# A four-layer decoder on one core: the first self attention's step order, and the last mixture's gather and buffers

## The reference, cut to what matters

```python
# first block: 16 heads of 64 features; x = x + this(layernorm(x))
q, k, v = x @ W_Q + b_Q, x @ W_K + b_K, x @ W_V + b_V      # per head
out = softmax(q @ k.T / 8) @ v;  out = sum over heads of out @ W_O + b_O

# last block: 32 experts, each takes its best cap = 70 of 1792 tokens
xe = xf[idx]                                   # gather: 70 tokens per expert
gate, upv = split(xe @ w_up.T)                 # 256 + 256 features
ye = (silu(gate) * upv) @ w_down.T
out = zeros.at[idx].add(w[..., None] * ye)     # weighted scatter-add
# and 16 adapters, one per two experts, on the same tokens, weighted by 0.05
```

## Time and profile before

| | us |
|---|---|
| median of 3 runs (lowest, highest) | 4221.11 (4218.85, 4239.77) |
| the profiled execution's own time | 4235.5 |
| its span | 4233.7 |
| first stage with its layer norm, up to the next one | 11.04 to 221.7 |
| the last stage's expert steps | 3951.0 to 4219.7 |

### The profile page before, as it was taken

One profiled execution on the slowest core, in us unless ns is written; L12 is line 12 of the kernel. 1 busy time (PEld: TensorE's weight loads), 2 busy tenths in 40 slices (PEclk: granted clock), 3 DMA queues, 4 the chain that ended last, 5 costly groups with the idle time before them and its releaser, 6 DMA issues. The chain is left out here.

```text
span 4233.7 us, 113113 instructions
## 1 busy us (share of the span) xinstructions
PE 3635.9 (86%) x48174; PEld 2505.2 (59%) x48174; DVE 2555.3 (60%) x4447; ACT 2097.0 (50%) x2832; POOL 1549.6 (37%) x1827
## 2 busy tenths in 40 slices
PE   7976459999997888799999988988899999972798
PEld 5654237777775446477777764434477777751565
DVE  4522568877774445578777753346688777746443
ACT  3344437666664232267666652344476666650010
POOL 1100037667661000267667620013466766610000
PEclk9998779999998899899999998989999999985897
DMA  4062045655651430456655621100465566510674
GB/s 147 2 253 102 2 108 148 151 145 148 157 140 37 98 85 3 96 137 152 152 142 150 157 50 55 54 8 9 105 150 147 141 156 150 143 42 0 159 184 123
DMA packets 203247, 464.39 MB, mean 110 GB/s; under 512 B 87486, under 2 KB 94398, under 8 KB 202590
## 3 DMA queue, kind: packets, MB, share of 16 engines
q1 hardware_dynamic: 200622, 455.30, 41.3%
q10 hardware_dynamic: 2160, 2.29, 0.2%
HBM read 212.72 MB, written 1.72 MB: 51 GB/s over the span
## 5 line engine op out<-in xcount | busy, mean ns | idle before, releaser
L1435 DVE TENSOR_REDUCE x_bank_top<-ps 112x1 f32<-112x500 f32 x2304 | 1418.7, 671 | 472.0 <-PE ps L1151 465.6
L1287 ACT ACTIVATE x_probs_t<-ps 128x1344 f32<-128x1344 f32 x768 | 991.2, 1291 | 215.0 <-PE ps L1168 210.4
L1168 PEld LDWEIGHTS ps<-x_queries,x_keys 128*128 128x128 bf16 x9216 | 488.7, 98 | 333.5 <-issue 152.9
L1151 PE MATMUL ps<-x_keys,x_queries 96*112 96x500 bf16 x2304 | 633.7, 381 | 25.0 <-DMA x_keys<-x_key_part 15.6
L1168 PE MATMUL ps<-x_queries,x_keys 128*128 128x112 bf16 x9216 | 585.4, 213 | 41.2 <-ACT x_probs_t L1287 36.6
L1181 PE MATMUL ps<-x_probs_t,x_values 128*32 128x112 f32 x18432 | 492.2, 263 | 5.3 <-ACT x_probs_t L1287 4.1
L1181 PEld LDWEIGHTS ps<-x_probs_t,x_values 128*32 128x32 f32 x18432 | 445.0, 111 | 70.1 <-issue 65.2
L1368 POOL TENSOR_TENSOR x_key_part<-x_key_whole,x_nothing 128x500 bf16<-128x500 f32 x270 | 336.8, 1247 | 259.3 <-ACT x_key_whole L1272 259.3
L1372 POOL TENSOR_TENSOR x_key_part<-x_key_left,x_nothing 128x500 bf16<-128x500 f32 x270 | 340.3, 1260 | 21.2
L1139 PE MATMUL ps<-x_wv,x_ctx_t 128*128 128x128 f32 (+1 forms) x2304 | 329.9, 287 | 9.8 <-issue 9.8
L1151 PEld LDWEIGHTS ps<-x_keys,x_queries 96*112 96x112 bf16 x2304 | 258.9, 131 | 127.9 <-DVE x_bank_top L1435 35.9
(11 more groups left out here) (455 smaller groups left out, 4526.8 us busy)
## 6 DMA issues: line engine op xcount, KB each, us to landing
x_keys<-x_key_part SPq DMA_DIRECT2D x1143, 192.0 KB, 3.7
x_ctx_t<-in_ctx_t SPq DMA_DIRECT2D x96, 750.0 KB, 6.1
cm_ctx_n<-in_ctx_n SPq DMA_DIRECT2D x32, 768.0 KB, 6.5
cm_ctx_t<-in_ctx_t SPq DMA_DIRECT2D x32, 750.0 KB, 8.7
e_share<-m_weight_scratch SPq DMA_DIRECT2D x32, 490.0 KB
e_spread_out<-m_slot_scratch SPq DMA_DIRECT2D x32, 490.0 KB
x_queries<-x_query_part SPq DMA_DIRECT2D x558, 28.0 KB, 2.7
e_share<-m_weight_rows SPq DMA_DIRECT2D x32, 448.0 KB, 5.8
```

What stands on the lines that cost most here:

```text
L1151: nc.tensor.matmul(ps[0:RW, n, 0:KB], queries[i // 2 % 2][0:TALL, p, i % 2, :], keys[i % 2][0:TALL, p, KB * n:KB * n + KB], start=True, st ...
L1168: mm = nc.tensor.matmul(ps[:, TURNED + c // VC, RW * (c % VC):RW * (c % VC) + RW], keys[i % 2][:, p, KT * c:KT * c + KT], queries[i // 2 % ...
L1287: nc.scalar.activation(probs_t[PROBS[p]].rearrange("k (n c) r -> k n (c r)", c=VC), ps[:, TURNED:TURNED + VR, 0:VC * RW], ACT.Exp, scale=s ...
L1435: nc.vector.tensor_reduce(bank_top[0:RW, p, n:n + 1], ps[0:RW, n, 0:KB], AX_X, ALU.max).then_inc(topped, 1)
```

## The change

In the first stage the layer norm moves inside the stage, the weight loads get three semaphores (queries and keys; values; output), and the order of a step becomes: turn(n), project, mix_values(n), make_scores(n + 2), make_values(n + 1), project_out. The mix gets two buffers. In the last stage there are three buffers for loads instead of two, the four spread rows are issued ahead of the weights, the loops are written out, and the gathered tokens are split into three bfloat16 parts whose sum is the float32 value. The marks are bfloat16, and the gather is 48 bfloat16 matmuls instead of 16 float32 ones. The parts are made during the router, by ACT copies and POOL subtractions.

```diff
 # self_attention_0, PE
-            pe.wait_ge(landed, 8 * 16)
+            for c in range(CH):
+                norm.centre(pe, c)
+            for c in range(CH):
+                norm.power(pe, c)
+            pe.wait_ge(qk_landed, 4 * 16)
             for t in range(TILES):
                 project(0, t)
+            pe.wait_ge(out_landed, 3 * 16)
+            pe.wait_ge(v_landed, 16)
...
-            for n in range(-1, NP_):
+            for n in range(-2, NP_):
                 if n >= 0:
                     turn(n)
-                if n + 1 < NP_:
-                    make_scores(n + 1)
-                if n > 0 and n % 2 == 0:
-                    project_out(n // 2 - 1)
                 for g, t in halves(n):
                     project(g, t)
                 if n >= 0:
                     mix_values(n)
-                if n + 1 < NP_:
+                if n + 2 < NP_:
+                    make_scores(n + 2)
+                if 0 <= n + 1 < NP_:
                     make_values(n + 1)
+                if n > 0 and n % 2 == 0:
+                    project_out(n // 2 - 1)
 # ACT
-            for n in range(-1, NP_):
+            for n in range(-2, NP_):
                 if n >= 0:
                     keep_turned(n)
                 for g, t in halves(n):
                     if t % 4 < 2:
                         keep_made(g, t)
-                if n + 1 < NP_:
-                    exponentials(n + 1)
+                if 0 <= n + 1 < NP_:
                     keep_values(n + 1)
+                if n + 2 < NP_:
+                    exponentials(n + 2)
 # DVE
+                for g, t in halves(n): keep_made      (t % 4 > 1)
+                if n >= 0: keep_mix(n)
+                if n + 2 < NP_: shift(n + 2), add_up(n + 2)
+                if n > 0 and n % 2 == 0: add(n // 2 - 1)
 # experts_by_slot
-    PAIRS, SUBS, LOADS = 16, 2, 6
+    PAIRS, SUBS, LOADS, DEEP = 16, 2, 6, 3
...
+            for n in range(PAIRS):
+                u = n % DEEP
+                if n >= DEEP:
+                    sp.wait_ge(used[u], n // DEEP)
+                for e in range(2):
+                    for dst, rows in ((share, weight_rows), (spread_out, slot_rows)):
+                        sp.dma_start(dst[u][:, e, :], ...to_broadcast([CAP, B * S])).then_inc(landed[u], 16)
+                sp.dma_start(w[u][:], ...); sp.dma_start(adapter[u][:], ...)
...
                 for t in range(NP_):
-                    mm = nc.tensor.matmul(..., by_token[:, t, :], marks[u][:, t]...)
+                    for k in range(PARTS):
+                        mm = nc.tensor.matmul(..., token_parts[k][:, t, :], marks[n % 2][:, t]...)
 # mixture_3
+            act.wait_ge(s["tokens_kept"], 2)
+            nc.scalar.copy(token_parts[0][:], tokens[:]).then_inc(s["part_kept"], 1)
...
             nc.scalar.copy(weight_rows[:], ...).then_inc(s["weights_kept"], 1)
+            for k in range(1, PARTS):
+                act.wait_ge(s["part_rest"], k)
+                nc.scalar.copy(token_parts[k][:], token_rests[k - 1][:]).then_inc(s["part_kept"], 1)
...
+        @block.gpsimd
+            pool.wait_ge(s["stats_ready"], 1)
+            for k in range(1, PARTS):
+                pool.wait_ge(s["part_kept"], k)
+                nc.gpsimd.tensor_tensor(token_rests[k - 1][:], whole[:], token_parts[k - 1][:], ALU.subtract)
```

More of the change, by code:

```diff
@@ L324, in project @@
                 if t % 4 == 1:
-                    wait(pe, added, g - 2 + t // 4)
+                    wait(pe, added, g - 2)
+                if t == 0 and g % 2 == 0:
+                    norm.wait_scaled(pe, max(g // 2, 1))
                 w = (wq, wk)[t // 4]
@@ L433, in keep_values @@
                 nc.scalar.copy(v[n % 2][:], ps[:, VALUES:VALUES + 2, :]).then_inc(v_kept, 1)
-            act.wait_ge(landed, 8 * 16)
+            nc.scalar.preload_act_table_set("natural_log")
+            for c in range(CH):
+                norm.square(act, c)
+            for c in range(CH):
+                norm.log(act, c)
+            for c in range(CH):
+                norm.inverse(act, c)
+            act.wait_ge(qk_landed, 4 * 16)
             for t in range(TILES):
@@ L494, in add @@
                                                ALU.add, ALU.add).then_inc(added, 1)
+            for c in range(CH):
+                norm.scale(dve, c)
+            for c in range(CH):
+                norm.wait_scaled(dve, c)
             nc.vector.memset(ps[:, SCORES:SCORES + 2, :], 0.0).then_inc(banks_clear, 1)
-            dve.wait_ge(landed, 8 * 16)
+            dve.wait_ge(qk_landed, 4 * 16)
             for t in range(TILES):
@@ L500, in _ @@
                     keep_made(0, t)
+            dve.wait_ge(out_landed, 3 * 16)
             dve.wait_ge(bias_done, 1)
             nc.vector.tensor_tensor(bo_sum[:], ps[:, VALUES, 0:1], bo[:], ALU.add).then_inc(bias_ready, 1)
[L503 to L507, removed]
+            for n in range(-2, NP_):
                 for g, t in halves(n):
@@ L1818, in experts_by_slot, with gather_bank, wait_landed @@
         GATE, UP = 5, 6
[L1820 to L1829, removed]
+        def gather_bank(n):
+            return (4, 7)[n % 2]
+        def wait_landed(engine, n):
+            engine.wait_ge(landed[n % DEEP], 16 * LOADS * (n // DEEP) + 16 * LOADS)
         block = own.enter_context(nc.Block(no_gpsimd_drain=True))
@@ L1835, in _ @@
                 sp.dma_start(dst[:], chip.dram[name]).then_inc(consts_landed, 16)
[L1836 to L1845, removed]
+            for n in range(PAIRS):
[4 more added lines that the diff above has]
+                    for dst, rows in ((share, weight_rows), (spread_out, slot_rows)):
+                        sp.dma_start(dst[u][:, e, :], rows[2 * n + e:2 * n + e + 1, :].to_broadcast([CAP, B * S])).then_inc(landed[u], 16)
+                sp.dma_start(w[u][:], chip.dram["L3_ffn_experts"][2 * n:2 * n + 2].rearrange("e p s m d -> p e s m d")).then_inc(landed[u], 16)
+                sp.dma_start(adapter[u][:], chip.dram["L3_ffn_adapters"][n:n + 1].rearrange("g p s m d -> (g p s) m d")).then_inc(landed[u], 16)
@@ L1867, in one_step @@
                 mm.then_inc(up_done, 1)
-                if more:
-                    gather(i + (u + 1) // 2, (u + 1) % 2)
+                if n + 1 < PAIRS:
+                    gather(n + 1)
                 pe.wait_ge(hidden_ready, n + 1)
@@ L1887, in _ @@
                 nc.tensor.matmul(ps[:, c, 0:CT], zero[:], chunk[c], start=True, stop=False, skip_group_check=True)
-            gather(0, 0)
-            all_steps(pe, one_step)
+            gather(0)
+            for n in range(PAIRS):
+                one_step(n)
             for c in range(CH):
@@ L1970, in mixture_3 @@
         by_token, square = sbuf("by_token", [P, NP_, P]), sbuf("square", [P, NP_, P])
+        tokens, token_rests = sbuf("tokens", [P, NP_, P]), [sbuf("token_rest%d" % k, [P, NP_, P]) for k in range(2)]
         stats = sbuf("stats", [P, NP_, NS])
@@ L2752, in decoder @@
             for stage in (self_attention_0, context_mixing):
-                normalise(chip, chip.x, chip.xn, True)
+                if stage not in NORMALISING:
+                    normalise(chip, chip.x, chip.xn, True)
                 stage(chip)
```

118 lines of the change are left out of this document (66 added, 52 removed).

## The result

| | before | after |
|---|---|---|
| median of 14 runs each (lowest, highest), us | 4222.33 (4211.89, 4239.77) | 4191.04 (4175.08, 4217.72) |
| ratio after / before (95% interval) | | 0.9927 (0.9909 to 0.9945) |
| profiled execution / span, us | 4235.5 / 4233.7 | 4186.23 / 4184.4 |
| start to the norm after the first stage | 221.8 | 207.2 |
| from there to the last stage's norm (same code) | 3565.0 | 3553.4 |

The kernel became faster by 31 us (0.7%), where 69 were forecast; 4191 lies above the range's 4182. The two profiles differ by 49, of which 11.5 lie in stages with the same code. That middle took 3553 to 3571 us in the fourteen kernels of this study, so a difference of a few us is read from the edited stages alone. There the profiles say -14.5 for the first stage (forecast -13.2) and -25.0 for the expert steps (forecast -53.6).

A forecast was written before the change was run, and what follows sets the result against it. PE was taken to bound the first stage's steady part; in the expert steps PE and DMA waited for each other. First stage -13.2 and last stage -55.5 gave -68.7 off the median 4221.1: 4152.4 us, range 4130 to 4182.

The forecast's parts named there:

- First stage, start: First stage up to turn(0): weights issued beside the norm start the projection 9.85 us earlier, of which -8.65 us is left.
- The steps: First stage's steps: the 0.69 us waits for POOL go, a pair takes 21.76 us instead of 22.04; -1.4 us in all.
- 1.01 wait on ACT: First stage, before the third tile: the step after an odd one loses 1.0 us to ACT's later eviction.
- the end: First stage, from turn(13) to the next norm: 24.4 us instead of 27.6, -3.2 us.
- Router parts: Last stage's router: ACT copies and POOL subtractions (about 4.7 us each) cost 0, at most +4.7 us.
- The gather: Last stage's expert steps: 48 bfloat16 matmuls at 61 ns take 2.93 us instead of 3.81, -0.88 us a step.
- Three buffers: Last stage's expert steps: loads get 26.7 us, PE sets 13.35 us a step against DMA's 13.0; 215.1 against 268.7, -53.6 us.
- the first rival: Last stage: DMA sets the step at about 15 us, total -46.7, 4174 us; chance 0.15.
- a sign of success: Last stage: DMA share was to rise from 0.64 to about 0.85 or more if the forecast held.

The follow-up runs named there:

- slots16: Kernel after, with slot rows stored and loaded as bfloat16 (2430 KiB a step instead of 2920): median 4164.29 us, ratio 0.9861 to the kernel before.
- mid_rows: Kernel after, with all four spread loads going to partitions 29 to 98 instead of 0 to 69: one execution, 4158.67 us.
- light_pe: Kernel after, with the scatter filling only one of four banks, so PE needs some 8.6 us a step: one execution, 4184.91 us.
- deep2: Kernel after, with two load buffers instead of three: median 4190.21 us, ratio 0.995 to the kernel before.

## Why the prediction failed, step by step

- **First stage, start: right in sum.** The projection started at 24.02, not 22.8. The weights were in; the norm itself ran 1.1 late, for its first eight matmuls took 6.29 instead of 4.96 and DVE's products began at 22.72 instead of 21.64. But the projection's first sixteen matmuls took 5.22 instead of 6.13. The scores came at 34.49 (forecast 34.2), turn(0) at 45.61 (forecast 43.8). The third tile went at 39.54, as forecast (39.4). The miss of 1.8 comes behind it: after that wait the granted clock averages 0.72 (39.5 to 45.6 us), and tiles, scores and values take 2.10, 1.76 and 2.42 where I had counted 1.5, 1.0 and 1.9.
- **The steps: right, a little better.** Pairs took 20.8 to 21.8 us, 21.4 on average (54.84 to 183.27 for six), forecast 21.76, with the forecast 1.01 wait on ACT. So turn(0) to turn(13) is 137.7 instead of the forecast 140.3, and the end 24.0 (183.27 to 207.24) instead of 24.4. That makes good the start's 1.8.
- **Router parts: right.** POOL's subtractions took 4.06 and 4.05 (estimate 4.7). The Trainium skill's rule of a lock between the two engines (SBUF — State Buffer, the paragraph on the shared port pair), weighed in the prediction, is for certain forms of instructions; this pair shows no delay. From one MAX8 to the next it is 4.16 us beside POOL's subtraction and 4.17 after it, in the timeline of the kernel after:

```profile
3851.85 4.05 POOL L2085 TENSOR_TENSOR m_token_rest<-m_token_rest,m_token_part 128x2048 f32<-128x2048 f32 x1 [42.81 <-ACT m_token_part L2074]
3853.17 2.02 DVE L2123 MAX8 m_row_top<-m_score_rows 32x8 f32<-32x1792 f32 x1
...
3857.33 2.02 DVE L2123 MAX8 m_row_top<-m_score_rows 32x8 f32<-32x1792 f32 x1
...
3861.50 2.02 DVE L2123 MAX8 m_row_top<-m_score_rows 32x8 f32<-32x1792 f32 x1
```

- **The gather: right in size, wrong in worth.** It took 2.93 us, 61 ns a matmul. It saves time only where PE is the bound; in the kernel after PE mostly is not.
- **Three buffers: the step that failed.** "So PE stays the bound, by 3%." The margin came from 230 GB/s (13.0 us a step), read in 26 us of the old kernel, when its first loads came in. With three buffers DMA moved 202 GB/s over 150 us. For 2920 KiB (2.99 MB) that is 14.8 us a step, and the steps after the first averaged 15.4. The forecast gave a load 26.7 us to land with three buffers; the last load of a step took 27 to 32. PE's side held: slots16 and mid_rows reach 215.7 and 214.9 us (forecast 215.1) once DMA has less to do or better places to write to. DMA's term was mis-sized: 13.0 stands where 14.8 to 15.4 belongs, and light_pe shows that DMA takes that long with PE out of the way. Its 26 us from 3936 on, at 246 GB/s, would have misled me too: the early rate does not last. Why packets are slow is shown only in part: source, place and load each move the number.
- **The rival.** The mechanism is the first rival's, "about 15", to which I gave 0.15. In the edited stages the profiles give -37.8 (without the middle's -11.5) where it said -46.7: the first stage did 1.3 better than counted there, and against it stand the first loads, which landed later (+4.1 in the router's row; deep2, with the same router, took 161.3 there, so this is what executions differ by), and steps of 15.4 instead of 15. The medians differ by -31; the other 6 lie within what executions differ.
- **What I should have seen.** The 230 GB/s came at a share of 0.87, so it looked as if there were room. That takes a packet's time as fixed: it was 239 ns before and 297 after. The share's rise to 0.94 stood in the prediction as a sign of success ("0.85 or more"); it was the sign of the bound.

## What to carry to other kernels

Read a DMA rate for a forecast from stretches as loaded and as long as in the new kernel, not from the start of a stage, and treat a margin of 3% between engine and DMA as a coin toss. When the DMA share is high, count time per packet as well as bytes: here packets to 70 partitions from 0 up took a third longer than packets of the same size placed across both halves (297 against 219 ns). When a load's time from issue to landing grows by as much as it is issued earlier, a deeper buffer buys nothing; take bytes away or place them better.

## What the runs showed of the hardware

- The same spread rows, at the same bytes, went with 297 ns a packet on partitions 0 to 69 and 219 on 29 to 98 (one execution, loaded tiles not read), and the steps took 243.5 and 214.9 us.
- Packets took 250 ns with two buffers of loads in flight and 297 with three (3960 to 4100 us), at 196 and 202 GB/s (3950 to 4100). With three and a DMA share of 0.94 they slowed from 247 to 318 ns within light_pe's expert steps.
- A bfloat16 matmul of 140 columns with its own weight load of 128x128 takes 61 ns in a row (48 in 2.93 us).
- POOL's 128x2048 float32 subtraction takes 4.05 us beside DVE's MAX8 rounds, which come every 4.16 us beside it and every 4.17 us after it.
